# Keys' low part directly behind the row maximum on VectorE, routing behind it; first tile's loads spread otherwise

## What is computed

```python
# 32 sequences of 256 x 256; attention with key = value = side
q = x + embed[stage][..., None]
attn = softmax(einsum('bsd,btd->bst', q, side))
o = einsum('bst,btd->bsd', attn, side)
# then, over all 8192 tokens: RMS norm, 8 experts of rank 16 on a shared FFN (D 256, F 1024)
t = o * rsqrt(mean(o * o) + eps) * norm_w
weights = two best of softmax(t @ gate_w.T), made to sum to 1
h1 = t @ w1.T + 2 * (t @ a1.T) @ b1.T         # per expert e; h3 with w3, a3, b3
act = silu(h1) * h3
out = x + sum_e weights[e] * (act @ w2.T + 2 * (act @ a2.T) @ b2.T)
```

## Time and profile before

| what | value |
|---|---|
| median of 3 runs | 1301.87 us (1301.62 to 1302.78) |
| profiled execution, its own time | 1303.9 us |
| its span, first to last instruction | 1302.1 us |
| PE busy | 1286.4 us (99% of the span) |
| DVE, ACT, POOL busy | 862.1, 532.0, 261.8 us |
| mean granted TensorE clock | 0.996 |
| stage 1, to the first matmuls of stage 2 | about 174 us |

### The profile page before, as it was taken

One profiled execution on the slowest core, in us unless ns is written; L12 is line 12 of the kernel. 1 busy time (PEld: TensorE's weight loads), 2 busy tenths in 40 slices (PEclk: granted clock), 3 DMA queues, 4 the chain that ended last, 5 costly groups with the idle time before them and its releaser, 6 DMA issues.

```text
span 1302.1 us, 18409 instructions
## 1 busy us (share of the span) xinstructions
PE 1286.4 (99%) x7078; PEld 1121.7 (86%) x7078; DVE 862.1 (66%) x1584; ACT 532.0 (41%) x991; POOL 261.8 (20%) x213
## 2 busy tenths in 40 slices
PE   9999899999999999999999999999999999999998
PEld 8989788888888888888888888888888888888887
DVE  6999656755775576656665667566675676575656
ACT  6878653333343334333333333333433343333332
POOL 2777640202020110202020202020020202020200
PEclk9999899999999999999999999999999999999999
DMA  8988821020202020201002020202020201102000
GB/s 274 229 222 224 212 75 32 3 73 1 74 2 73 2 73 2 73 1 49 26 19 56 1 74 2 73 2 73 2 73 1 58 17 37 38 1 73 1 17 17
DMA packets 121248, 76.55 MB, mean 59 GB/s; under 512 B 63162, under 2 KB 112200, under 8 KB 121032
## 3 DMA queue, kind: packets, MB, share of 16 engines
q1 hardware_dynamic: 120848, 75.35, 20.8%
q10 hardware_dynamic: 312, 0.02, 0.0%
HBM read 58.21 MB, written 17.14 MB: 58 GB/s over the span
## 4 chain that ended last, share of the span: by engine, by line
PE 92%; DVE 3%; SPq 2%; DMA 1%; issue 1%; POOL 1%; ACT 0%; DVEq 0%; POOLq 0%
PE bank L1346 30%; PE bank L1345 30%; PE bank L1347 30%; PE bank L1469 1%; DMA k_pair<-in_fside_BxSxS 1%; DVE neg_max L1016 0%; PE bank L1453 0%; PE bank L1391 0%; POOL value_lo L636 0%; PE bank L1357 0%; DVE bank L989 0%; DVE probT_lo L1021 0%; DMA kv<-in_fside_BxSxS 0%; DVE q L982 0%; SPq L523 0%
## 5 line engine op out<-in xcount | busy, mean ns | idle before, releaser
L1217 DVE TENSOR_TENSOR act_a<-silu_a,bank 128x512 f32<-128x512 f32 x128 | 87.7, 685 | 211.6 <-PE bank L1347 195.0
L866 ACT ACTIVATE br_hi<-act_br 128x512 fp32r<-128x512 f32 x128 | 80.9, 632 | 187.7 <-DVE act_br L1228 187.7
L859 ACT ACTIVATE silu_b<-bank 128x512 f32<-128x512 f32 x128 | 76.2, 595 | 187.9 <-PE bank L1347 187.1
L683 POOL TENSOR_TENSOR t_lo<-t_in,t_hi 128x512 fp32r<-128x512 f32 x32 | 40.6, 1289 | 552.5 <-ACT t_hi L846 552.3
L1346 PE MATMUL bank<-w2T_lo,s_hi 128*128 128x256 f32 x512 | 144.7, 283 | 0.0
L1347 PE MATMUL bank<-w2T_hi,s_lo 128*128 128x256 f32 x512 | 143.3, 280 | 0.0
L1345 PE MATMUL bank<-w2T_hi,s_hi 128*128 128x256 f32 x512 | 142.7, 279 | 0.0
L1225 DVE TENSOR_TENSOR act_b<-silu_b,bank 128x512 f32<-128x512 f32 x128 | 88.0, 687 | 80.9 <-PE bank L1347 80.0
L855 ACT ACTIVATE silu_a<-bank 128x512 f32<-128x512 f32 x128 | 75.7, 591 | 134.8 <-PE bank L1347 134.7
L702 POOL TENSOR_TENSOR v_lo<-v_full,v_hi 128x512 fp32r<-128x512 f32 x64 | 94.5, 1510 | 136.6 <-ACT v_hi L851 136.6
L1238 DVE TENSOR_TENSOR br_lo<-act_br,br_hi 128x512 fp32r<-128x512 f32 x128 | 104.8, 818 | 5.3 <-ACT br_hi L866 2.8
(11 more groups left out here) (204 smaller groups left out, 3234.6 us busy)
## 6 DMA issues: line engine op xcount, KB each, us to landing
kv<-in_fside_BxSxS SPq DMA_DIRECT2D x32, 256.0 KB, 3.6
t_scratch<-oT SPq DMA_DIRECT2D x32, 256.0 KB, 3.2
t_in<-t_scratch SPq DMA_DIRECT2D x32, 256.0 KB
x_out<-in_x SPq DMA_DIRECT2D x16, 512.0 KB, 3.9
out<-x_out SPq DMA_DIRECT2D x30, 256.0 KB, 4.1
x_pair<-in_x SPq DMA_DIRECT2D x52, 128.0 KB, 3.3
k_pair<-in_fside_BxSxS SPq DMA_DIRECT2D x52, 128.0 KB, 3.3
rho<-scale_scratch SPq DMA_DIRECT2D x16, 256.0 KB
```

What stands on the lines that cost most here:

```text
L859: nc.scalar.activation(silu_b[:, :], h1_bank[j % 2][:, :], ACT.Silu).then_inc(silu_b_ready, 1)
L866: nc.scalar.activation(br_hi[j % 2][:, :], act_br[j % 2][:, :], ACT.Copy).then_inc(br_hi_ready, 1)
L1217: nc.vector.tensor_tensor(act_a[j % 2][:, :], silu_a[j % 2][:, :], h3_bank[j % 2][:, :], ALU.mult).then_inc(act_a_ready, 1)
```

## The change

Two things change; the computation stays the same, and no operation or DMA is added or taken away.

1. On DVE, in every step `beside(c-1)` now stands behind `k_low(c+1)` instead of ahead of it.
2. On SP, the first tile's loads are split in two groups. `t_in` of both sequences and `rstd` get the semaphore `scaled_loaded` and are issued one behind each of the steps 23, 24 and 25. The routing rows are stored behind step 22. The masks and `rho` are issued together behind step 28. `beside(27)` waits for `scaled_loaded`, and `mask_u(0)` waits for the masks and `rho`.

```diff
-        TILE_LOADS = 16 * 6
+        TILE_LOADS, SCALED_LOADS = 16 * 6, 16 * 3
...
         ROWS_STEP = ROUTE_STEP + 10
-        TILE_STEPS = range(ROWS_STEP + 1, ROWS_STEP + 6)
+        FIRST_ROWS_STEP = ROWS_STEP + 2
+        SCALED_STEPS = range(FIRST_ROWS_STEP + 1, FIRST_ROWS_STEP + 4)
+        MASK_STEP = BATCH - 4
...
-            def load_tile_part(k):
+            def load_scaled_part(k):
                 if k == 0:
                     sp.wait_ge(wT_ready, JOBS)
                     for p in range(2):
                         sp.wait_ge(t_stored[p], 32)
-                    load_t_seq(0, 0)
-                    store_rows(0)
-                if k == 1:
-                    load_t_seq(0, 1)
                 if k == 2:
                     sp.wait_ge(rows_stored, 32)
-                    load_masks(0)
-                if k == 3:
-                    load_scale(0, 0)
-                if k == 4:
                     load_scale(0, 1)
+                else:
+                    load_t_seq(0, k)
...
             for c in range(ROWS_STEP, BATCH):
                 step(c)
-                if c in TILE_STEPS:
-                    load_tile_part(c - TILE_STEPS[0])
+                if c == FIRST_ROWS_STEP:
+                    store_rows(0)
+                if c in SCALED_STEPS:
+                    load_scaled_part(c - SCALED_STEPS[0])
+                if c == MASK_STEP:
+                    load_masks(0)
+                    load_scale(0, 0)
...
                 if c == T0_STEPS[0]:
-                    wait_tile(0, buffer_used=False)
+                    dve.wait_ge(scaled_loaded, SCALED_LOADS)
                     scale_t(0, 0)
...
                 if c != 1:
                     row_max(c)
-                if c >= 1:
-                    beside(c - 1)
                 if c + 1 < BATCH:
                     if c + 1 not in TURNED:
                         q_low(c + 1)
                     k_low(c + 1)
+                if c >= 1:
+                    beside(c - 1)
...
                 if first:
                     dve.wait_ge(value_lo_ready, BATCH)
+                    dve.wait_ge(tile_loaded[0], tile_count(0))
```

More of the change, by code:

```diff
@@ L254, in adaln_moe_ffn @@
         rows_stored = sem("rows_stored")
+        scaled_loaded = sem("scaled_loaded")
         tile_loaded = sems("tile_loaded", 2)
@@ L401, in out_count, with tile_count @@
             return 16 * sum(KT if k == TILES - 1 else 2 for k in range(c % 2, c + 1, 2))
+        def tile_count(c):
+            return TILE_LOADS * (c // 2 + 1) - (SCALED_LOADS if c % 2 == 0 else 0)
         def group_in(c):
@@ L530, in load_t_seq @@
                 sp.dma_start(t_in[c % 2][:, b].rearrange("p c s -> p (c s)"), t_seqs[2 * c + b]
-                             ).then_inc(tile_loaded[c % 2], 16)
+                             ).then_inc(tile_loaded[c % 2] if c else scaled_loaded, 16)
             def load_masks(c):
@@ L540, in load_scale @@
                 row = scale_scratch[w, bass.ds(KT * c, KT)].rearrange("k n -> (k n)")
-                sp.dma_start((rho, rstd)[w][c % 2][:, :], row.partition_broadcast(P)).then_inc(tile_loaded[c % 2], 16)
+                sp.dma_start((rho, rstd)[w][c % 2][:, :], row.partition_broadcast(P)
+                             ).then_inc(tile_loaded[c % 2] if c or w == 0 else scaled_loaded, 16)
             def load_tile(c):
@@ L1126, in scale_t, with wait_tile @@
                     ins.then_inc(t_scaled_ready, 1)
[L1128 to L1131, removed]
+            def wait_tile(c):
+                dve.wait_ge(tile_loaded[c % 2], tile_count(c))
+                dve.wait_ge(t_lo_ready, c)
             def load_weight(c, buffer_used=True):
```

## The result

| | before | after |
|---|---|---|
| median | 1302.39 us (6 runs, 1301.62 to 1304.32) | 1294.12 us (6 runs, 1291.79 to 1297.2) |
| profiled execution, its own time | 1303.9 us | 1292.7 us |
| its span | 1302.1 us | 1290.9 us |

The ratio is 0.9937 (95% interval 0.992 to 0.9954): the changed kernel is faster by 0.6%, some 8.3 us by the medians and 11.2 us by the two profiled executions. The three longest of its six executions (1295.14, 1296.65 and 1297.2 us) have mean granted clocks of 0.999, 0.997 and 0.997, the three shortest 0.999 to 1.0. The changed kernel was run again in three later comparisons; its medians were 1291.94, 1291.0 and 1294.18 us, those of the kernel before in the same comparisons 1302.52, 1301.59 and 1302.89 us, which are gains of 10.6, 10.6 and 8.7 us.

A forecast was written before the change was run, and what follows sets the result against it. PE bounds the kernel, except DVE in routing steps and late `k_pair` DMAs in steps 24 to 27. Terms 2.3 + 0.7 + 0.6 + 0.5 + 9.5 - 1.5 = 12.1 us, then 2.0 off, gave 1289.8 us; range 1287.0 to 1296.5.

The forecast's parts named there:

- rival 1: Steps 22 to 27: transfers stay late, stalls of 4 to 8 us, clock falls once; 1293 to 1297 us, chance 0.20.
- Offset to the median: Whole run: the profiled execution lies 2.0 us above the median, so 1291.8 became 1289.8 us.
- Routing behind the low part: Steps 11 to 18, DVE: low part fills the first routing operation's wait for POOL; gain 2.3 us (0.8 to 2.9).
- Low clock in step 12: Step 12: PE's wait splits into two of about 0.9 us and the clock holds; gain 0.7 us, else 0.
- Step 20: Step 20, DVE: L1118 was 1.0 us over its normal time; gain 0.6 us (low end 0.2).
- Steps 28 and 29: The two scalings: step 29 wins 0.5 to 0.9 us, step 28 costs 0.3 to 0.4; net gain 0.5 us.
- Loads: Steps 24 to 27: with no `k_pair` late, they fall from 26.34 to 16.8 us; gain 9.5 us.
- new stalls: `k_pair` of steps 25 and 27 late behind `t_in` and `rstd`; cost 1.5 us (0 to 4.7).
- The low DMA share of the earlier trace: From 136 to 145 us: share of 0.67, read as masks loading on 8 engines, 2.2 us for 1.1; changed no term.
- the order gains nothing: Steps 11 to 29: POOL may catch the routing again; gain 0 to 1 us, 1292.5 to 1294 us, chance 0.08.
- the fourth rival: Step 27: a stall of 8 to 10 us merely moves to its `k_pair`; 1299.5 to 1304 us, chance 0.05.
- the fifth: Steps 26 and 28: `k_pair` late, clock falls behind both, kernel slower; 1304.5 us or more at 16 us, chance 0.03.

The follow-up runs named there:

- third profile: The kernel before, unchanged, run and profiled once more; 1299.51 us (1 run).
- turn-first run: Kernel before, with q's transpose directly behind the maximum, ahead of the routing, in steps 11 to 29; 1300.45 us, ratio 0.9986.
- masks moved: Kernel before, with the two masks alone loaded behind step 28 with their own semaphore; 1297.39 us, ratio 0.996.
- order only: Kernel before, with routing placed behind the keys' low part on DVE and the loads left as before; 1297.42 us, ratio 0.9966.
- fourth profile: The changed kernel, unchanged, run and profiled again in a later comparison; median 1294.18 us (5 runs).
- loads only: Changed kernel with `beside` put back ahead of the low parts, so only the loads are spread; 1296.5 us, ratio 0.9963.

## Why the prediction was right, and where it was off

The forecast was 1289.8 us, range 1287.0 to 1296.5. The measured 1294.12 lies inside the range, but 4.3 us above the forecast, outside the band of 1288.2 to 1292.5 to which I gave 0.58, and inside that of rival 1, to which I gave 0.20. The gain was 8.3 us where the sum had 12.1. The medians of the three later sets, 1291.94, 1291.0 and 1294.18, lie twice in the one band and once in the other. All 20 executions of the changed kernel run from 1290.82 to 1297.2 us and have their middle at 1292.5: the forecast is 2.7 us too low against that, and too low for every single execution. So the mechanisms held, and the width of the range covered two terms that were sized wrong.

**Offset to the median: the step that failed.** The sum gave 1291.8 us from the profiled execution's own time, and I took 2.0 us off since that execution lay 2.0 above its median. That was wrong: its excess lay largely in the stretches that the change mends. Its steps 24 to 30 were 0.7 and 3.2 us longer than in the two later profiles, its steps 11 to 20 0.6 us. The terms were priced from that execution, so they hold this excess already, and taking it off the sum once more counts it twice. By 12.1 us from the own time alone the forecast would have been 1291.8.

**Routing behind the low part, 2.3 us.** Right in mechanism and a little small. Against the two profiles of before in which the clock held, steps 11 to 18 are shorter by 0.58, 0.19, 0.59, 0.19, 0.39, 0.20, 0.40 and 0.19 us (third profile less after), 2.7 us. The alternation is what I had forecast, a full gain in one step and a smaller one in the next. What I wrote ahead of it, that moving an operation inside a full queue gains nothing by itself, holds for the kernel before: in its third profile no maximum in steps 11 to 18 waits for the scores. It doesn't hold once the cover has made DVE's work shorter: in the turn-first run the scores came too late for DVE in steps 13 to 18 and 20, steps 13 to 20 are 0.8 us longer than in the changed kernel, and the clock took some 1.5 us more.

**Low clock in step 12, 0.7 us.** Right for the profile; as a term of the median too large. In both later profiles of before PE waited 1.82 us at the same place, the clock held and step 12 took 4.46 us, not 5.41. The changed order has no such wait: the two pieces that I took for 0.9 us each were 0.24 and 0.70.

**Step 20, 0.6 us.** Measured 0.58 (5.18 to 4.60); L1118, now L1124, went from 1172 to 586 ns.

**Steps 28 and 29, 0.5 us.** Step 29 won 1.0 (5.15 to 4.16), but in the later profiles of before it took 4.29 and 4.78 us. Step 28 is hidden under the new wait: L1129's mean of 843 ns, less 0.67 us for the one in step 29, leaves 1.02 us for the first scaling: it met POOL and cost 0.3 us, as I wrote, though by its times (147.2 to 148.2) it met the `x_pair` add (146.58 to 147.6) and not `qT_lo`. POOL's next `qT_lo`, started while the scaling ran, took 1.73 us in place of 1.29, so the waiting goes the other way too:

```profile
147.17 1.02 DVE L1129 TENSOR_TENSOR t_in<-t_in,rstd 128x512 f32<-128x512 f32 x1
```

```profile
147.59 1.73 POOL L655 TENSOR_TENSOR qT_lo<-q,qT_hi 128x512 fp32r<-128x512 f32 x1
```

**Loads, 9.5 us, and new stalls, 1.5 us.** In the profile 9.42 us, and 1.6 us given back in step 28. Over three profiles of before and four of after, steps 24 to 30 take 39.6, 38.9 and 36.4 us against 30.8, 31.5, 29.8 and 33.9: 38.3 less 31.5, 6.8 us on average. I had 9.5 - 1.5 + 0.5 = 8.5. By these few profiles the term is too large by 1.7 us. It was priced from the longest stretch of the three, and neither the stalls nor the clock behind them are constants of this kernel: the half clock stood for 6.8 us in the first profile (steps 26 and 27), for 6.8 in the second (3.4 in step 26, 3.4 in steps 28 and 29) and not at all in the third; of the four after only the fourth had it, for 3.4. It is the same error as the offset, seen in its place. The price by bytes was too low for the masks: 1.1 us for their 0.25 MB, where moving them alone won 4.2. The low DMA share of the earlier trace rows, which I had put beside their shape, is in all three profiles of before: in the 9 us that begin 6.3 us ahead of that `k_pair`'s issue it was 0.67, 0.72 and 0.82, and 1.00 in the same stretch with the masks moved. I had let that sign change no term; it bore on the masks' price.

**The opening.** Step 11 starts 1.6 us later in the profile after. The POOL operation `q` (L666) waited 6.4 us there for the first `x_pair`, issued at about 28 us, long before anything in the change. The start of step 11 lies between 68.6 and 72.0 us in all profiles, at 68.7 to 69.7 in the six with the low part behind the routing and 68.6 to 72.0 in the eight with it ahead. `beside` holds nothing before step 11, so the order of work in steps 1 to 10 is the same in both; where the difference comes from stays open. The sum had no term for it.

**The rivals.** That the order gains nothing is refuted by order only. That the transfers stay late came true in part, in some executions: after's fourth profile (1295.85 us) has 16.4 us in steps 28 to 30 and 3.4 us at half clock, and two of the six executions of the result had a mean clock of 0.997 and took 1296.65 and 1297.2 us. What held them can't be seen, as they were not profiled. No execution of the changed kernel reached the 1299.5 us from which the fourth rival, or the fifth, would have begun.

## What to carry to other kernels

Where an operation of one engine waits for the running instruction of another, the order is worth time even if the queue is full: put an operation that keeps its normal length beside the other engine's instruction in that place, and choose the one whose result the bound engine waits for. Gains of a few tenths of a microsecond from dodging such a meeting don't add up, since each shorter step moves the meeting of the next. And a profiled execution's excess over the median is no offset: ask first in which stretch it lies, if need be with a second profile, before a term is priced from that stretch.

## What the runs showed of the hardware that was not expected

The same wait of PE brings the clock down or doesn't. In loads only PE waited 1.82 us, and the 3.4 us behind it, where the earlier trace rows has 0.50, ran at full clock:

```profile
73.52 0.36 PE L1351 MATMUL bank<-kT_hi,qT_hi 128*128 128x256 f32 x1 [1.82 <-DVE kT_lo L1006]
```

```profile
74.90:78.30 3.40, 3.40 (x29) 3.18 (x28) 3.30 (x13) 2.83 (x9) 1.65 (x2) 1.00 0.74 168
```

Of six profiles with this wait, the half clock (1.2 GHz) followed in three, each time for 3.4 us, and the full clock (2.4 GHz) stayed in three. Where it fell, it did so 1.5 us behind the end of the wait (the kernel before, first profile), 0.6 us (turn first) and 0.7 us (masks moved). What decides it stays open.
